# Layer 2a of a graph kernel: the leaky activation as a linear part by TensorE and an absolute value by ScalarE

## The reference

```python
xl = (x @ Wl + bl).reshape(N, heads, out_ch)
xr = (x @ Wr + br).reshape(N, heads, out_ch)
e = jax.nn.leaky_relu(xl[src] + xr[dst], NEG_SLOPE)        # NEG_SLOPE = 0.2
logits = jnp.einsum('ehc,hc->eh', e, att)
m = jax.ops.segment_max(logits, dst, num_segments=N)
ex = jnp.exp(logits - m[dst])
denom = jax.ops.segment_sum(ex, dst, num_segments=N)
alpha = ex / denom[dst]
out = jax.ops.segment_sum(xl[src] * alpha[..., None], dst, num_segments=N) + bias
```

## Time and profile before

| what | value |
|---|---|
| time, median of 3 runs | 4844.04 us (4839.3 to 4848.83) |
| the profiled execution | 4839.3 us, span 4837.6 us |
| busy over the span | PE 79%, PEld 53%, DVE 75%, ACT 66%, POOL 64% |
| mean granted TensorE clock | 0.935 of full speed |
| layer 2a | about 2965 to 3548 us of the span |

### The profile page before, as it was taken

The page is one execution under the profiler, slowest core; times in us unless marked ns, Lnnn a source line. Parts: engine busy times, 40 slices in busy tenths (PEclk is TensorE's granted clock), DMA queues, the critical chain, the costliest instruction groups (busy, mean ns, idle before and its releaser), DMA issues. The chain is left out here.

```text
span 4837.6 us, 74788 instructions
## 1 busy us (share of the span) xinstructions
PE 3813.0 (79%) x19896; PEld 2560.8 (53%) x20115; DVE 3637.8 (75%) x5894; ACT 3183.7 (66%) x10636; POOL 3089.0 (64%) x3645
## 2 busy tenths in 40 slices
PE   3888888888888699999688886888867777576676
PEld 3666666666666456666465564555534444344444
DVE  3666566666666488888599996999979999577776
ACT  2888888888887578888588885555545555333333
POOL 4889898898998577777444442333234443477775
PEclk9999999999999799999799998999989999788888
DMA  2334334334433333333233332333334433333221
GB/s 68 103 106 109 106 104 112 105 109 111 111 107 95 99 85 94 91 89 82 69 87 88 90 89 63 106 106 107 96 77 107 107 107 89 84 83 83 82 80 48
DMA packets 695838, 451.77 MB, mean 93 GB/s; under 512 B 143539, under 2 KB 623257, under 8 KB 695696
## 3 DMA queue, kind: packets, MB, share of 16 engines
q1 hardware_dynamic: 219504, 182.41, 14.0%
q10 hardware_dynamic: 413392, 186.30, 13.5%
q0 software_dynamic: 62800, 81.68, 7.0%
HBM read 253.00 MB, written 199.90 MB: 94 GB/s over the span
## 5 line engine op out<-in xcount | busy, mean ns | idle before, releaser
L769 POOL TENSOR_TENSOR node_rstd<-node_variance,minus_half 128x4 f32<-128x4 f32 x588 | 650.1, 1109 | 13.5 <-DMA slot_map<-node_value,node_index 1.4
L224 ACT ACTIVATE node_z<-psum 128x128 f32<-128x128 f32 x1960 | 513.5, 277 | 156.7 <-PE psum L204 87.6
L230 DVE TENSOR_TENSOR node_x<-psum,node_rstd 128x512 f32<-128x512 f32 x294 | 202.9, 690 | 487.2 <-POOL node_rstd L769 487.2
L1153 POOL DMA_INDIRECT slot_src_rows<-x,slot_index x392 | 450.8, 1150 | 168.5 <-issue 104.5
L919 POOL DMA_INDIRECT slot_map<-node_value,node_index x392 | 417.6, 1065 | 74.5 <-issue 73.5
L224 ACT ACTIVATION_READ_ACCUMULATOR node_z<-psum 128x1 f32 x1960 | 407.0, 208 | 0.0
L224 ACT ACTIVATE slot_logit<-psum 128x128 f32<-128x128 f32 x980 | 256.7, 280 | 198.0 <-PE psum L204 197.9
L1153 POOL DMA_INDIRECT slot2b_src_rows<-xl,slot2b_index x196 | 249.1, 1271 | 81.8 <-issue 46.2
L213 PE MATMUL psum<-ident,node_x 128*128 128x128 f32 x784 | 140.0, 306 | 193.9 <-DVE node_x L230 193.4
L1139 POOL DMA_INDIRECT out_nodes<-slot_new,slot_side_index x196 | 228.0, 1163 | 91.6 <-POOL slot_side_index L1133 43.8
L204 PE MATMUL psum<-center,slot_t 128*128 128x128 f32 x1176 | 215.1, 285 | 81.5 <-DVE slot_t L1592 52.7
(11 more groups left out here) (400 smaller groups left out, 12778.7 us busy)
## 6 DMA issues: line engine op xcount, KB each, us to landing
x<-node_x ACTq DMA_DIRECT2D x294, 256.0 KB, 2.7
slot_keep<-keep SPq DMA_DIRECT2D x147, 256.0 KB, 3.9
node_xT<-in_x_T SPq DMA_DIRECT2D x98, 256.0 KB, 3.4
out_nodes<-node_x ACTq DMA_DIRECT2D x98, 256.0 KB, 3.0
x<-slot_new ACTq DMA_DIRECT2D x98, 256.0 KB, 2.4
slot_dst_rows<-x SPq DMA_DIRECT2D x98, 256.0 KB, 4.3
staged<-node_gathered ACTq DMA_DIRECT2D x14, 896.0 KB, 5.9
xl<-node_xl ACTq DMA_DIRECT2D x98, 128.0 KB, 3.8
```

The costliest lines, as they stand in the source:

```text
L224: ins = act.activation(g.z[u][:, t, :], rows[:, t, :], ACT.Square, scale=float(D ** -0.5), accum_out=g.mean_square[u][:, t:t + 1])
L230: v.tensor_tensor(out[:, :, :], source, g.rstd[u][:, :].unsqueeze(2).broadcast_to([P, TILES, D]), ALU.mult)\
L769: pool.tensor_tensor(g.rstd[u][:, :], g.variance[u][:, :], g.c.minus_half[:, :], ALU.pow).then_inc(g.pool_out[u], 1)
L1153: pool.indirect_dma_start(src_rows[u][:, t, 0:src_width], None, table, at_index(index[u][:, t:t + 1], 0))\
```

## The change

With x = z + bias, max(0.2 x, x) = 0.6 x + 0.4 |x|. The logit's difference is linear in both parts, and in the linear part the two activations share a term: 0.6 S1 (z − zo) = 0.6 S1 (Wl1 xs − Wl1 xd), where the bias falls out. So

- ACT z and zo write |z + bias| (function Abs in place of Identity).
- DVE z and zo are gone.
- PE r has four products in place of two: `slope1` with xs, `minus_slope1` with xd, `S1` with t1 and `minus_S1` with t2, the last two with weights times 0.4. It waits for ACT zo, not for DVE zo.
- `prepare` makes `slope1` and `minus_slope1`: one more transpose, one more product, and on DVE one more copy from PSUM, two scalings from PSUM and two in SBUF.
- The 2a entry of `PLAN` is another table, with a period of 11.20 in place of 11.51 and other starts for all steps.

```diff
-        "2a": (11.51, (11.024, 6.110, 7.042, 11.029, 8.744, 14.775, 15.025, 15.897, 16.472, 15.661, 15.666, 19.070,
...
+        "2a": (11.20, (5.903, 7.962, 7.967, 15.301, 16.374, 19.827, 19.842, 24.613, 24.618, 24.209, 28.101, 29.668,
...
             v.tensor_copy(WT[:, :], psum[:, 0, 0:D]).then_inc(worked, 1)
+            v.tensor_copy(Wl1T[:, :], psum[:, 1, 0:D]).then_inc(worked, 1)
...
+            v.tensor_scalar(c.slope1[:, :], psum[:, 6, 0:D], STRAIGHT, None, ALU.mult).then_inc(worked, 1)
+            v.tensor_scalar(c.minus_slope1[:, :], psum[:, 6, 0:D], -STRAIGHT, None, ALU.mult).then_inc(worked, 1)
...
+            v.tensor_scalar(c.S1[:, :], c.S1[:, :], BENT, None, ALU.mult).then_inc(worked, 1)
+            v.tensor_scalar(c.minus_S1[:, :], c.minus_S1[:, :], BENT, None, ALU.mult).then_inc(worked, 1)
...
+            pe.transpose(psum[:, 1, 0:D], c.Wl1[:, :], c.ident[:, :])
...
-                                   (4, raw["Wn"], S["a_tgt"], D), (5, raw_edge, S["a_edge"], EF)):
+                                   (4, raw["Wn"], S["a_tgt"], D), (5, raw_edge, S["a_edge"], EF), (6, Wl1T, c.S1, D)):
...
-        "2a": [("DVE", "dst"), ("PE", "z"), ("PE", "zo"), ("ACT", "z"), ("ACT", "zo"), ("DVE", "z"), ("DVE", "zo"),
-               ("PE", "r"), ("PE", "v")],
+        "2a": [("DVE", "dst"), ("PE", "z"), ("PE", "zo"), ("ACT", "z"), ("ACT", "zo"), ("PE", "r"), ("PE", "v")],
...
+                    if layer == "2a":
+                        act_copy(act, g, u, t1[u][:, :], A(u), ACT.Abs, c.blr1[:, 0:1])
...
-                    act_copy(act, g, u, t2[u][:, :], B(u), ACT.Identity, c.blr1[:, 0:1])
+                    act_copy(act, g, u, t2[u][:, :], B(u), ACT.Abs, c.blr1[:, 0:1])
...
-                    pe.wait_ge(*g.DVE.done(u, i, "zo"))
-                    product(u, A, [(c.S1[:, :], first), (c.minus_S1[:, :], second)])
+                    pe.wait_ge(*g.ACT.done(u, i, "zo"))
+                    product(u, A, [(c.slope1[:, :], src), (c.minus_slope1[:, :], dst), (c.S1[:, :], first), (c.minus_S1[:, :], second)])
```

More of the change, by code:

```diff
@@ L47 @@
 SLOPE = 0.2
+STRAIGHT, BENT = 0.5 * (1.0 + SLOPE), 0.5 * (1.0 - SLOPE)
 NODE_STREAMS = 7
@@ L335, in prepare @@
     c.pair_src, c.pair_dst, c.pair_gap = sb("pair_src", [P, D]), sb("pair_dst", [P, D]), sb("pair_gap", [P, D])
+    c.slope1, c.minus_slope1 = sb("slope1", [P, D]), sb("minus_slope1", [P, D])
     c.Wl2r2, c.Wlin1 = sb("Wl2r2", [P, D]), sb("Wlin1", [C2 + 1, D])
@@ L388, in prepare @@
     WT = temp("W_transposed", [P, D])
+    Wl1T = temp("Wl1_transposed", [P, D])
     map_rows = 125
@@ L544, in _ @@
             v.tensor_copy(WT[:, :], psum[:, 0, 0:D]).then_inc(worked, 1)
-            n += 1
+            v.tensor_copy(Wl1T[:, :], psum[:, 1, 0:D]).then_inc(worked, 1)
+            n += 2
             v.wait_ge(products, 2)
@@ L549, in _ @@
             v.tensor_copy(c.Wedge[:, :], psum[0:EF, 5, 0:D]).then_inc(worked, 1)
-            n += 5
+            v.tensor_scalar(c.slope1[:, :], psum[:, 6, 0:D], STRAIGHT, None, ALU.mult).then_inc(worked, 1)
+            v.tensor_scalar(c.minus_slope1[:, :], psum[:, 6, 0:D], -STRAIGHT, None, ALU.mult).then_inc(worked, 1)
+            n += 7
             v.wait_ge(worked, n)
+            v.tensor_scalar(c.S1[:, :], c.S1[:, :], BENT, None, ALU.mult).then_inc(worked, 1)
+            v.tensor_scalar(c.minus_S1[:, :], c.minus_S1[:, :], BENT, None, ALU.mult).then_inc(worked, 1)
             v.tensor_copy(c.self_src[:, 0:C2], c.Wsa[:, 0:D:2]).then_inc(worked, 1)
@@ L554, in _ @@
             v.tensor_tensor(c.self_dst[:, C2:], c.Wsa[:, 0:D:2], c.Wda[:, 0:D:2], ALU.add).then_inc(worked, 1)
-            v.wait_ge(worked, n + 3)
+            v.wait_ge(worked, n + 5)
             v.wait_ge(counted, 3)
@@ L587, in _ @@
             pe.matmul(psum[:, 7, 0:D], all_ones[0:C2, :], c.Wlin[:, :], start=True, stop=True)
+            pe.transpose(psum[:, 1, 0:D], c.Wl1[:, :], c.ident[:, :])
             pe.transpose(psum[:, 0, 0:D], c.W[:, :], c.ident[:, :]).then_inc(products, 1)
-            pe.wait_ge(worked, 25 + 7 + 14 + 3 + 10 + 5 * 8 + 1)
+            pe.wait_ge(worked, 25 + 7 + 14 + 3 + 10 + 5 * 8 + 2)
             for b, lhs, rhs, m in ((1, WT, S["att_src"], D), (2, WT, S["att_dst"], D), (3, raw["Wn"], S["a_src"], D),
-                                   (4, raw["Wn"], S["a_tgt"], D), (5, raw_edge, S["a_edge"], EF)):
+                                   (4, raw["Wn"], S["a_tgt"], D), (5, raw_edge, S["a_edge"], EF), (6, Wl1T, c.S1, D)):
                 ins = pe.matmul(psum[0:m, b, 0:D], lhs[:, :], rhs[:, :], start=True, stop=True)
@@ L1224, in work @@
                     act.wait_ge(*g.PE.done(u, i, "z"))
-                    act_copy(act, g, u, t1[u][:, :], A(u), ACT.Identity, (c.blr1 if layer == "2a" else c.pair_bias)[:, 0:1])
+                    if layer == "2a":
+                        act_copy(act, g, u, t1[u][:, :], A(u), ACT.Abs, c.blr1[:, 0:1])
+                    else:
+                        act_copy(act, g, u, t1[u][:, :], A(u), ACT.Identity, c.pair_bias[:, 0:1])
                 elif step == "zo":
                     act.wait_ge(*g.PE.done(u, i, "zo"))
-                    act_copy(act, g, u, t2[u][:, :], B(u), ACT.Identity, c.blr1[:, 0:1])
+                    act_copy(act, g, u, t2[u][:, :], B(u), ACT.Abs, c.blr1[:, 0:1])
                 elif step == "l":
```

## The result

The changed kernel takes 4867.16 us, the median of 5 runs (4863.89 to 4869.47), and the kernel before 4842.07 us beside it (4839.3 to 4848.83, 5 runs). The ratio is 1.0048, with a 95% interval of 1.0033 to 1.0063: slower by about 23 us, which is 4865 us by the ratio (4842.07 × 1.0048). The forecast was 4865. The profiled execution of the changed kernel took 4869.47 us, with a span of 4867.8 and a mean clock of 0.935, the same clock as before.

The account below looks back on a forecast made before the run. A circle of waits through ScalarE and TensorE bounds layer 2a: +0.35 us over 47 turns gives +16.5, preparation +1.2, fill and drain +3, total +20.7; from the median of before, 4844.04, that is 4865 us. Range 4849 to 4880.

Parts of the forecast that it names:

- What bounds, and what leaves VectorE: Layer 2a: VectorE alone sets the pace at 11.09 us a turn; losing z and zo (1.21) leaves it 9.88.
- TensorE's load of 11.03 us: Layer 2a: TensorE's 9.31 us a turn plus two products, 1.72; even a perfect order gains only 0.06 per turn.
- The circle: Layer 2a: waits through ScalarE's zo to exps and TensorE's tot to zo, 11.44 us a turn; chance 0.66.
- dear case: Layer 2a: waits dearer than summed, hand-over to zo 0.18 more, srcT 0.06; 11.6 to 11.7 a turn, 4876 us; chance 0.14.
- The sum: Whole kernel: turns +16.5, preparation +1.2, fill and drain +3, total +20.7 us.
- The drain: Fill and drain of layer 2a: a longer last chain, products at half the clock; +3 us, between 0 and +7.
- the preparation: Before the turns: one more product counts as well as five small VectorE steps; +1.2 us, between 0.5 and 1.9.
- a sign against itself: Outside layer 2a: a difference of more than 3 us would put the whole forecast beside the point.
- TensorE's load sets the pace: Layer 2a: this or a second circle through VectorE, 11.03 to 11.15 a turn, 4845 to 4851 us; chance 0.17.
- VectorE still sets the pace: Layer 2a: 9.88 us a turn, 4791 us, if packed products take TensorE less than 0.86; chance 0.03.

Follow-up runs that it names:

- e3: The changed kernel with ScalarE's exps moved right behind exp in its order; 11.02 us a turn, ratio 1.0000 to the kernel before.
- e5: The changed arithmetic in the order of before, without TensorE's wait for its stream's stores ahead of the source transposes; 11.03 us a turn, ratio 1.0019.
- e12: The changed kernel without TensorE's wait for its stream's stores ahead of the source transposes; 11.59 us a turn, ratio 1.0061.
- e9: The changed kernel without the two linear products of r, in the order of before; 10.54 us a turn, ratio 0.9981.
- e1: The changed arithmetic in the order of before, without the entries of VectorE's z and zo; 11.88 us a turn, ratio 1.0122.
- e2_no_linear: The changed kernel and its order without the two linear products of r; 12.87 us a turn, ratio 1.0167.
- e8: The changed kernel without the two linear products of r and with exps right behind exp; 10.99 us a turn, ratio 0.9969.

## Why the prediction was right

**What bounds, and what leaves VectorE.** VectorE went from 45.00 to 40.26 of 45 us. Its two steps are gone, and it waits 0.52 us for exps and 0.25 to 0.47 ahead of den.

**TensorE's load of 11.03 us** was right to 0.01 (e3 and e5), and so was the judgement that even a good order gains almost nothing. The Trainium skill ("Perfetto Trace Analysis", section "Identifying the Most-Contended Engine") names two measures of TensorE's headroom, the share of the peak FLOPs that the kernel reaches and the weight loads' busy share. The prediction took up the second alone, and read by itself it misleads here: in e3 the loads are busy 26.38 of 45 us, 59%, and TensorE has no idle time. The first was not worked out here.

**The circle** was right in its place and its members. The terms, as measured in the changed kernel, beside the sum's:

| term | predicted | measured |
|---|---|---|
| ScalarE, zo to the end of exps | 5.50 | 5.59 (3120.62 to 3126.21) |
| hand-over to tot, with its slower start | 0.05 + 0.06 | 0.15 + 0.02 |
| TensorE, tot to the end of zo | 5.79 | 5.79 |
| hand-over to ScalarE | 0.04 | 0.04 |
| sum | 11.44 | 11.59 |

The 0.09 on ScalarE is its srcT: I took 0.52 from its like, neg, and it takes 3122.76 − 3122.15 = 0.61. The prediction named that as a part of its dear case, and of the 0.15 it makes more than half. The mean turn, 11.57, lies between the forecast circle's 11.55 and the dear case's 11.6.

**The sum.** Layer 2a was to give 19.5 us and gave 22. The turns gave 18.0 where 16.5 was forecast: 0.48 instead of 0.35 each, which the first three turns partly gave back. The drain gave 4.0 instead of 3, and the preparation 1.6 instead of 1.2; the node pass's first memset starts there:

```profile
66.58 0.15 DVE L885 MEMSET node_raw<- 128x1 f32 x4 [0.58 <-PEq L401]
```

against 64.98 before. The fill changed by −0.1. Together that is 23.5 us where 20.7 was predicted, and the ratio says 23. What is left of the two profiled spans' 30.2 is the 6.6 us in stages that run the same instructions. The size of the steady turn's step was off by 0.13 us, the term of ScalarE's srcT and the hand-over to tot; that the 4865 comes so near to the median is in part luck, since the median of before that it was added to fell by 2 us with more runs.

The prediction named a sign against itself: a difference outside layer 2a of more than 3 us. The two profiled spans have 8.2 there, 1.6 of it the preparation. The sign was set too tight, since the other 6.6 lie in stages with the same instructions, whose time differs by more than that between traces. What carries the mechanism is not the span but e3, where one number of the order takes the whole 0.5 us a turn away, and e12, where taking out the store wait changes nothing.

**The rivals.** "TensorE's load sets the pace" failed for the kernel as it stands and is exactly true with one number of its table changed. "VectorE still sets the pace" failed, and e9 shows that in the order of before it would have failed even with products that cost nothing (10.54 us, not 9.88). The missing piece of the analysis was the wait of the source transposes for the stores. It doesn't bind in the changed kernel (e12), but in the order of before the change costs 0.80 us a turn (e1) instead of 0.48.

## What to carry to other kernels

Work taken from a full engine and given to another is worth the smaller of the two rooms, and then what the orders leave of it: sum the engines' loads first, then follow each in-order queue around until it closes, with every DMA issue and landing on it. A wait that is free today (the store wait under VectorE's 11.08 us) binds as soon as the cover gets shorter, so removing load and removing that wait were worth 0.5% together and nothing measurable apart. Half a removal was the better trade here: one VectorE step and one product instead of two products.

## What was not expected of the hardware

TensorE's clock. In e2_no_linear, with 1.72 us less work a turn for TensorE, idle pieces of 2.0 to 2.1 us by the rows were followed by 3.4 us at 1.2 GHz in three turns of four (3189.4 to 3192.8 around the second window above), and the kernel was slower by 1.3 us a turn than with the work left in. The changed kernel (pieces of 0.38 us), e9 (0.9 to 1.1), e8 (1.0 to 1.3) and the kernel before (1.40) stayed at 1.00 in the steady windows. Why the fourth piece of the same 2.09 us brings no fall stays open. These are rows of five kernels and no rule: no run varied the length of an idle piece alone.
